# A chunked delta-rule layer with a mixture of experts: the core of one step beside the inverse of the next

## The reference, cut to what matters

```
q, k, v = silu(conv4(x @ Wq)), silu(conv4(x @ Wk)), silu(conv4(x @ Wv))
beta    = sigmoid(x @ Wb);   q, k = l2norm(q), l2norm(k)
per head and chunk:  M = eye + tril(k_beta @ k.T, -1);  u = M^-1 v_beta;  w = M^-1 k_beta
per chunk in order:  u = u - w @ S
                     o = q @ S + tril(q @ k.T) @ u
                     S = S + k.T @ u
o = rmsnorm(o) * onorm_w
```

## Time and profile before

| | us |
|---|---|
| median of three runs | 1058.81 |
| the profiled execution | 1065.67 |
| its span | 1063.9 |
| PE busy | 834.1 (78%) |
| DVE busy | 665.1 (63%) |
| ACT busy | 367.5 (35%) |
| granted TensorE clock, mean | 0.912 |

### The profile page before, as it was taken

One profiled execution on the slowest core, in us unless ns is written; L12 is line 12 of the kernel. 1 busy time (PEld: TensorE's weight loads), 2 busy tenths in 40 slices (PEclk: granted clock), 3 DMA queues, 4 the chain that ended last, 5 costly groups with the idle time before them and its releaser, 6 DMA issues. The chain is left out here.

```text
span 1063.9 us, 31221 instructions
## 1 busy us (share of the span) xinstructions
PE 834.1 (78%) x13520; PEld 634.8 (60%) x13520; DVE 665.1 (63%) x1267; ACT 367.5 (35%) x683; POOL 117.5 (11%) x182
## 2 busy tenths in 40 slices
PE   6586697895899799889889879186882899999910
PEld 5565576773568577567567756154452787887800
DVE  2698598796679878878877967933138122222226
ACT  2533435523534542553452552122220122222215
POOL 2000000000000000000000000000001445445244
PEclk9887698998999999999999999599796899999965
DMA  8110002007001100300200100100105799999768
GB/s 270 72 43 2 4 1 83 4 1 245 24 4 41 63 4 1 102 4 2 81 23 2 62 23 3 47 36 2 60 29 228 270 363 362 356 345 372 237 145 239
DMA packets 48626, 113.16 MB, mean 106 GB/s; under 512 B 8576, under 2 KB 8704, under 8 KB 48368
## 3 DMA queue, kind: packets, MB, share of 16 engines
q1 hardware_dynamic: 42224, 96.50, 25.0%
q0 software_dynamic: 6272, 14.68, 6.4%
HBM read 84.34 MB, written 26.84 MB: 104 GB/s over the span
## 5 line engine op out<-in xcount | busy, mean ns | idle before, releaser
L463 PE MATMUL bank<-xnT,wring 128*128 128x256 f32 x768 | 168.6, 381 | 0.0
L463 PEld LDWEIGHTS bank<-xnT,wring 128*128 128x128 f32 x768 | 145.8, 191 | 23.7 <-issue 3.3
L1592 PEld LDWEIGHTS ps_g<-xgT,wring 128*128 128x128 f32 x1024 | 120.8, 194 | 17.2 <-issue 17.2
L1592 PE MATMUL ps_g<-xgT,wring 128*128 128x128 f32 x1024 | 121.3, 277 | 1.3 <-ACT xgT L1622 1.3
L996 DVE SCALAR_TENSOR_TENSOR cv<-pre,taps,cv 128x1024 f32<-128x1024 f32 x72 | 92.3, 1282 | 22.6 <-ACTq L754 21.2
L1725 DVE TENSOR_TENSOR hid<-ps_g,sg 128x160 f32<-128x160 f32 x32 | 10.4, 324 | 148.3 <-ACT sg L1632 148.3
L1501 POOL MEMSET xgT<- 128x512 f32 x2 | 1.0, 532 | 785.7 <-POOLq L1803 785.7
L596 PE MATMUL bank<-hT,sg_w 128*128 128x256 f32 x256 | 69.0, 407 | 1.7 <-issue 1.7
L1622 ACT ACTIVATE xgT<-ps_x 128x320 f32<-128x320 f32 x32 | 14.0, 437 | 160.6 <-PE ps_x L1581 160.6
L606 PE MATMUL bank<-sd_w,sh_h 128*128 128x512 f32 x128 | 64.0, 630 | 0.9 <-DVEq L1117 0.9
L596 PE MATMUL bank<-hT,su_w 128*128 128x256 f32 x256 | 63.2, 390 | 1.8 <-issue 1.8
(11 more groups left out here) (189 smaller groups left out, 1401.7 us busy)
## 6 DMA issues: line engine op xcount, KB each, us to landing
wring<-in_ffn_W_gate SPq DMA_DIRECT2D x32, 512.0 KB, 8.6
wring<-in_ffn_W_up SPq DMA_DIRECT2D x32, 512.0 KB, 10.1
wring<-in_ffn_W_down SPq DMA_DIRECT2D x32, 512.0 KB, 11.6
x_in<-in_attn_x SPq DMA_DIRECT2D x8, 512.0 KB, 3.8
x_res<-in_attn_x SPq DMA_DIRECT2D x8, 512.0 KB, 4.5
x_rows<-x SPq DMA_DIRECT2D x8, 512.0 KB, 2.9
h_rows<-h SPq DMA_DIRECT2D x8, 512.0 KB, 3.8
side_rows<-acc_sb SPq DMA_DIRECT2D x8, 512.0 KB, 5.2
```

The costliest lines, as they stand in the source:

```text
L463: m = te.matmul(bank[:, c * COLS:(c + 1) * COLS], wqkv[:, w, kt, ct * P:(ct + 1) * P], xnT[:, kt, :], start=(kt == 0), stop=(kt == KT - 1))
L1592: m = te.matmul(ps_g[q % 2][:, (2 * a + i) * P:(2 * a + i + 1) * P], w[:, k, i * P:(i + 1) * P], xgT[q % 2][:, k, :], start=(k == 0), stop ...
```

## The change

The pipeline is one step deeper, with other work in each body. In body s the engines do: the core of step s-1; the grams, masks and inverse of step s, for which betas are computed in body s too; the projections and transposes of x of step s+1; output projection, rows and transposes of h of step s-2; routing, second half of the shared up product and shared down product of step s-3. The first half of shared up (E) of step s-2 closes body s. There are bodies 0 to 10.

`kq` and `v_tok` have two buffers, by the parity of the step. `grams` holds the key grams once and the query grams twice. `invT` and `k_tok` keep one buffer; `turn_k` now stands behind the last `next_state` of a body. All loops over steps are unrolled, all steps are plain numbers, and the increments of `pe_passed` and `sp_passed` are gone. The ring's numbering is read off one table of PE's order instead of one by phases.

PE's order, and the table of the ring:

```diff
-SIZE = dict(X=2, P=6, H=2, V=1, Y=1, E=2, F=1, I=1, O=2, G=4, W=2)
-LAG = dict(P=0, G=0, X=-1, O=1, W=1, H=2, E=2, F=2, I=2, V=3, Y=3)
-
-ORDER = dict(begin="XPGX", one="PXOGW", two="PHEXFOGIW", loop="PHVYEXFOGIW", seven="PHVYEFOGIW", end="HVYEFIOWVYHEFIVY")
+PIECES = dict(X=1, H=1, O=1, G=4, P=12, W=8, E=8, F=8, V=4, Y=4)
+BANKS = dict(X=2, H=2, O=2, G=4, P=6, W=2, E=2, F=2, V=1, Y=1)
+
+FILL = ["BXRWW", "WWW", "WWW", "PP", "GPP", "GFF", "GFF", "GFF", "FF", "HP", "P", "PP", "VVVV", "YY", "YY", "PPPPOEEEEEEEE"]
+FILLS = {0: ["BGGGGXPPPPPPPPPPPP"], STEPS + 1: ["RWWWWWWWWFFFFFFFFVVVVYYYYH"], STEPS + 2: ["REEEEEEEEFFFFFFFFVVVVYYYY"]}
+
+
+def step_of(body, section):
+
+    if section in "XP":
+        return body + 1
+    if section in "BG":
+        return body
+    if section == "O":
+        return body - 1
+    if section in "WH" or (section == "E" and body < STEPS + 2):
+        return body - 2
+    return body - 3
+
+
+def pieces_of(body):
+
+    done = dict.fromkeys("BRXHOGPWEFVY", 0)
+    slots = []
+    for letters in FILLS.get(body, FILL):
+        slot = []
+        for c in letters:
+            if 0 <= step_of(body, c) < STEPS and not (body == STEPS + 1 and c == "E"):
+                slot.append((c, step_of(body, c), done[c]))
+                done[c] += 1
+        slots.append(slot)
+    return slots
+
+
+def all_jobs():
+
+    order = [("X", 0, n) for n in range(BANKS["X"])] + [("P", 0, n) for n in range(BANKS["P"])]
+    for body in range(STEPS + 3):
+        for slot in pieces_of(body):
+            for c, step, n in slot:
+                if c in "BR":
+                    continue
+                if PIECES[c] == 1:
+                    order += [(c, step, b) for b in range(BANKS[c])]
+                elif n % (PIECES[c] // BANKS[c]) == 0:
+                    order.append((c, step, n // (PIECES[c] // BANKS[c])))
+    return {job: n for n, job in enumerate(order)}
+
```

In this table B is the betas, R the router, and G, P, W, E, F, V and Y are issued in pieces: a P is half a bank, a W one of four accumulating products, a V or Y one of four. F now stands for both banks (gate and up) of the second half. PE's program is then:

```diff
+        for body in range(STEPS + 3):
+            if 0 <= body - 1 < STEPS:
+                core(body - 1, fill_for(body))
+            else:
+                fill_for(body)(0)
```

The buffers, and the masks that fill them (the grams' layout was chunk, kind, column and is now kind, chunk, column):

```diff
-    kq = sb("kq", [P, G, 2, CH])
+    kqs = [sb(f"kq{n}", [P, G, 2, CH]) for n in range(2)]
-    v_tok = sb("v_tok", [P, G, DK])
+    v_toks = [sb(f"v_tok{n}", [P, G, DK]) for n in range(2)]
-    grams = sb("grams", [P, G, 2, CH])
+    grams = sb("grams", [P, 3, G, CH])
...
+        def masks(s, j):
+
+            ring.wait_full(dve, "G", s, j)
+            bank = ring.bank("G", s, j)[:, :].rearrange("p (i a c) -> p a i c", i=I8, a=2)
+            both = grams[:, 0:2 + s % 2:1 + s % 2, :, :].rearrange("p a (i j) c -> p j a i c", j=J)[:, j]
```

SyncE's order: per body the betas, x two steps ahead, the zeroing of `side_rows` (in body 2), rows, residual, shared rows:

```diff
-        for t in range(STEPS):
-            sp.dma_start(side_d[0:NTOK, :].rearrange("(b t p) d -> t p b d", p=TT, b=B)[t], acc_sb[:, :, :]).then_inc(side_zero, 16)
-        sp.dma_start(side_d[NTOK:NTOK + CAP, :], acc_sb[0:CAP, 0, :]).then_inc(side_zero, 16)
-        with sp.Fori(2, STEPS - 2) as s:
-            load_x(s + 2)
-            load_residual(s)
-            shared_out(s - 2)
-            rows(s)
-            move_beta(s + 2)
+        for s in range(STEPS + 3):
+            if s < STEPS:
+                move_beta(s)
+            if s + 2 < STEPS:
+                load_x(s + 2)
+            if s == 1:
+                load_residual(0)
+            if s == 2:
+                for t in range(STEPS):
+                    sp.dma_start(side_d[0:NTOK, :].rearrange("(b t p) d -> t p b d", p=TT, b=B)[t], acc_sb[:, :, :]).then_inc(side_zero, 16)
+                sp.dma_start(side_d[NTOK:NTOK + CAP, :], acc_sb[0:CAP, 0, :]).then_inc(side_zero, 16)
+            if 0 <= s - 2 < STEPS:
+                rows(s - 2)
+            if 0 < s - 1 < STEPS:
+                load_residual(s - 1)
+            if 0 <= s - 3:
+                shared_out(s - 3)
```

More of the change, by code:

```diff
@@ L662, in _ @@
-        body(1, "one")
-        body(2, "two")
-        with pe.Fori(LOOP_FROM, LOOP_TO) as s:
-            body(s, "loop")
-        body(STEPS - 1, "seven")
-        turn_h(STEPS - 2, "end")
-        core(STEPS - 1, "end", filler(STEPS, "end"), STEPS, STEPS - 1)
-        for q in range(4):
-            shared_up(STEPS - 2, "end", "F", 1, q)
-        output_squares(STEPS - 1, "end")
-        out_proj(STEPS - 1, "end")
-        for b in range(B):
-            for ft in range(FT):
-                shared_down(STEPS - 2, "end", b, ft, nth=1)
@@ L1302, in _ @@
-        body(1, "one")
-        body(2, "two")
-        with dve.Fori(LOOP_FROM, LOOP_TO) as s:
-            body(s, "loop")
-        body(STEPS - 1, "seven")
-        for j in range(J):
-            residual(STEPS - 1, j)
-            if j == 2:
-                route_scores(STEPS - 2)
-                route_groups(STEPS - 2)
-            next_state(STEPS - 1, j)
-            if j == 2:
-                hidden(STEPS - 2, "end", 0)
-        route_experts(STEPS - 2)
-        output_sums(STEPS - 1)
```

751 lines of the change are left out of this document (339 added, 412 removed).

## The result

| | before | after |
|---|---|---|
| median of four runs each, us | 1059.64 (1057.84 to 1062.69) | 1045.14 (1041.81 to 1046.42) |
| ratio of the two | | 0.9855, 95% interval 0.9822 to 0.9889 |
| profiled execution, us | 1065.67 | 1041.81 |
| its span; step part; expert part | 1063.9; 792.6; 271.3 | 1040.1; 768.8; 271.3 |

The change makes the kernel 1.5% faster, 14.5 us; forecast were 36. Against the forecast for the profiled execution (1029.6) the miss is 12.2 us, and all of it lies in the step part (768.8 against 756.5).

The account below looks back on a forecast made before the run. Two engines near full wait in turn: DVE floor 76.6 us a body, PE about 76. Prologue 92.5, bodies 73, 72, 3 x 82, 80, 78, tail 115 sum to 756.5 against 792.6, 36 less: profiled 1029.6, median 1023, range 1003 to 1054.

Parts of the forecast that it names:

- Body 3, 97.1 to 82: Body 3: issuing the side_rows zeroing at the start of body 2 removes ACT's 11.9 us wait; 97.1 to 82 us.
- Bodies 4 to 6, 82, 82 and 80: Steady bodies: the new order removes waiting, floors stay; 82 us for bodies 4 and 5, 80 for body 6.
- It costs nothing if PE's own round stays under the DVE's: Steady bodies: PE's first projection piece waits for the shared gate's bank from 8 to about 11.5 us, at no cost.
- the DVE's remaining waits: Steady bodies: mean shift 1.4, state of chunk 2 1.9 through ACT's key norms, small ones 1; 4.3 us on 76.6.
- PE's pauses, 6.5 to 2.5: Steady bodies: pauses read as PE outrunning its instruction blocks between small groups; fills cut them from 6.5 to 2.5 us.
- Body 2, 72: Body 2: DVE work 63.4, plus 3.8 between instructions and 4.5 of waits; 72 us, was 84.6.
- Prologue, +3: Prologue: the first norm of step 2 is added on the DVE; with a wait for ACT, 3 us longer.
- Tail, 115: Tail: body 8 at 55, bodies 9 and 10 at 55, cold clock 5; 115 us, was 96.7.
- the clock: Rival, 12%: PE falls to 1.2 GHz in thinner bodies; bodies 1, 2, 7 and tail cost 8 + 5 + 4 + 5 more: 1045.
- PE is the bound: Rival, 18%: PE's busy time and pauses remain and fills meet new waits; bodies 3 to 7 stay near 86: 1053.
- The ring turns into a chain: Rival, 10%: fixed bank order makes PE's first projection piece wait 3.5 us for the shared gate's bank; 90 a body, 1086.
- my own signs of error: Wrong if a steady body exceeds 85 us, PE waits over 4 with DVE idle, or bodies 2 to 6 clock under 0.95.

Follow-up runs that it names:

- the zeroing alone: Kernel before the change, with only the transfers that zero side_rows issued ahead of the first rows: 1054.1 us, ratio 0.9924.
- the useless work: Changed kernel, with PE computing the second output projection twice in bodies 3 to 6: 1041.2 us, ratio 0.9807 to the kernel before.
- both repaired: Changed kernel plus shared hidden products ahead of the convolutions and both moves in ACT's order: 1031.9 us, ratio 0.9715 to the kernel before.
- all edits together: Changed kernel plus early hidden products where convolutions follow, both ACT moves, betas first, spread projection pieces: 1027.3 us, ratio 0.9676 to the kernel before.

## Why the prediction was right and wrong

The sign was right and the median of 1045.1 lies in the range of 1003 to 1054, but the size was off: less than half of the 36 us. Of the 22 us between the forecast median and the measured one, 12 are in the step part below; the other 10 are that the profiled execution of before, from which the forecast worked, lies 6 to 7 us above its median and the one after 3.3 below. Step by step, by the windows of the profiled executions:

*Body 3, 97.1 to 82* (82.9 measured): right in size and cause. The wait for `side_rows` went, nothing took its place, and the zeroing alone makes 10 us of it in the old kernel.

*Bodies 4 to 6, 82, 82 and 80* (85.8, 85.8, 83.6): wrong, and 11 of the 12 us of miss. (That the rest adds up to 1 is luck: prologue, body 2 and body 3 came out 3.3, 4.7 and 0.9 worse, bodies 1 and 7 and the tail 1.2, 1.6 and 5.0 better.) Two terms failed. "It costs nothing if PE's own round stays under the DVE's" was the sentence for PE's wait at the shared gate's bank. The wait came as forecast: at 8.7 us into the body PE had nothing left to do, and the bank was free at 12. That it costs nothing as a wait is shown by the useless work. But it took PE's clock down: the 16 products behind it took 1.7 us more, and with the second dip, behind PE's wait for the residual, the body came out 3.3 to 3.7 us longer, nearly all of it as waits of the DVE for L485 and L507. I had priced the clock for bodies 1, 2, 7 and the tail, by their long idle stretches, and let the steady bodies keep their 1.00. The second term was the DVE's remaining waits, 4.3 us in the forecast (1.4 mean shift, 1.9 state, 1 small). They were 3.2 + 3.4 + 1.3 and about 1 of small ones, 8.9. The mean shift's was named with its right cause and mis-sized; moving ACT's norm ahead removes it and 2 to 3 us of the body. The state's cause was named wrong: not ACT's key norms but PE, 1.6 us of it by the low clock. With both repaired the DVE waits 2.0 + 1.3 + 1, and the bodies are at 81.3 to 81.8. That this is 4.3 again is in part luck: the mean shift no longer waits, and the 1.3 is for ACT's sigmoid, which the forecast did not count. So the floors (71.9 busy + 4.7 between instructions) and the way to 82 were sound, for an order that the change doesn't have.

*PE's pauses, 6.5 to 2.5*: they fell to 0.4. The Trainium skill, "Runtime: NRT & Kernel Launch", "Instruction fetch mechanics", calls the crossing of a block of 256 instructions mostly hidden; were that so here, the pauses had to be something else and to stay at 6.5. They went with the order of the groups, and they are such crossings: 254 and 256 instructions apart, each ending 2.1 to 2.9 us after a packet set out. So the crossing is hidden in most places of the changed kernel, as the page has it, and not where a block holds little but small products. My reading of them was right, my condition (two groups without a wide one between) wrong: one pair doesn't do it. As a term of the time they changed no body by what they last: 3.3 us added came mostly out of a wait that was there, and 3.0 removed shortened one wait of the DVE by 1.9 and lengthened another by 2.0.

*Body 1, 73* (71.8) and *body 7, 78* (76.4): a little better than forecast. *Body 2, 72* (76.7): wrong by 4.7. I had costed it by the DVE alone. Its waits there are 4.3 for the state, 1.6, 1.6 and 1.3, where the forecast had 4.5 in all; ahead of the first stands PE with two pauses of 2.3 us and a clock of 0.60 around the second. With pauses alone taken away the first wait fell by 1.9 us and the one at the mean shift grew by 2.0; all edits together gave 2.6; the rest is open.

*Prologue, +3* (+6.3): the first norm of step 2 was counted; that the betas of step 0, moved behind the projections, put three ACT passes in front of the first sigmoid was not, nor that the projections themselves take 1.8 us longer than before without them in front (23.6 against 21.7). Undoing it gives 92.2, against the 92.5 of the forecast.

*Tail, 115* (110.0): 5 us better, exactly the term for the cold clock, which read 0.95 here. Other executions of the same tail, at 0.91, took 113.1 and 114.4.

*Unrolling and SP's moved transfers at nothing*: right as far as seen. The expert part is 271.3 in both; instruction packets fell from 111 to 104; nothing waits for x, residual or rows.

Of the rivals, *the clock* came true in part, and in bodies where I had not looked for it: its 12% was for 1045 by other stretches. *PE is the bound* (18%, 1053) would also have left the steady bodies at 86, but its reason is refuted: PE with 3.5 us more work made the kernel faster. *The ring turns into a chain* named the very wait, at 3.5 us; its consequence, 90 us a body, did not come. Two of my own signs of error did show: steady bodies over 85 us, and a clock under 0.95 in body 2.

## What to carry to other kernels

When an engine's wait is costed at nothing because it has slack, price also what the idle time does to its clock: in this kernel 3.5 us of harmless waiting cost 3.3 to 3.7 us a body, and filling it with useless products was as good as removing it in two of three bodies (3.3 us each; 1.3 in the third, where the clock fell behind a later wait). Before a pipeline is rebuilt, move the single late transfer that the waits name: here it was half of the gain by itself. After the rebuilding look at the order on each engine again, since the instruction that sets the end is another one.

## What the runs showed of the hardware that I had not expected

- PE idle for 3.5 us between two dense stretches: the granted clock of the following 6 us is 0.72, and 16 products of 128x128 by 128x256 take 5.38 us instead of 3.69. With the gap filled it stays 1.00. In 24 of 24 bodies with such a wait the products behind it were slow, yet a wait of 2.99 us in the tail was followed by 1.00 in one execution and by 0.50 in another. The Trainium skill, "TensorE: Matmul & The Clock Gate", "HAM oscillation — how this bites in real kernels", says that waits between groups of products throttle PE over and over; the trace agrees, and shows it in a body in which PE is busy for 78 of 86 us.
- The same tail, with the same order on every engine, took 110.0 to 114.4 us in different executions, the two longest with a granted clock of 0.91 and the others with 0.95 or more.
- PE's pauses inside groups of identical small products stand at the ends of blocks of its instructions: 127 or 128 products with their weight loads from one to the next in a stretch of small groups, and 2.1 to 2.9 us from the setting out of a 16 KB packet to the end of each of the 47 pauses counted above. They last up to 2.6 us in these profiles, and where a block holds wide products they are short or absent: a wide piece of about 1 us, as the kernel before had, left 1.28 us of one.
